# Linear attention on one core: denominators over nine columns, and numerators written into the state's PSUM bank

## The chip, the cores and the metric

The kernel runs on one NeuronCore of a Trainium2 chip. The metric is the time of the device in microseconds (us), the median of several runs. Engines are named as in the profile: PE (TensorE, matmuls), PEld (its weight loads), DVE (VectorE), ACT (ScalarE), POOL (GpSimd), SP (SyncE, which here only starts DMAs). L12 is line 12 of the kernel before. One execution was also recorded by the hardware profiler, and all rows come from it.

## What is computed

An input of 16 x 256 tokens with 128 features goes through a causal linear attention with 16 heads of 8 features, a residual with a layer norm around it, and then a mixture of experts with one expert chosen for each token. The change touches the attention alone. Of the reference:

```
q = elu(x @ Wq + bq) + 1 ;  k = elu(x @ Wk + bk) + 1 ;  v = x @ Wv + bv
def step(carry, qkv):
    s, z = carry
    s = s + einsum('bhd,bhm->bhdm', k_i, v_i)
    z = z + k_i
    qs = einsum('bhd,bhdm->bhm', q_i, s)
    qz = einsum('bhd,bhd->bh', q_i, z)[..., None]
    return (s, z), qs / (qz + 1e-06)
```

So each token has 128 numerators `qs` and 16 denominators `qz + 1e-06`.

## The kernel before, in words

The 4096 tokens are 32 tiles of 128 (token on the partition). A sequence of the batch is two tiles, an even one and an odd one, and the sums over time start anew with each even tile. The attention stage is an unrolled software pipeline over the tiles `t`; each engine runs its own list `step1(t, u)`, `u = t % 4`, in order, and semaphores alone tie the lists together. For tile `t`:

- ACT norms the tile (`xn`), copies the transposed tile out of PSUM (`xnT`), and after the projection makes the parts of elu (`neg`, `rl`, `ex`) and `v`.
- POOL adds them to `qk` (L446) and multiplies every k with every v of its head to `kv`, 128 x 1024 (L452).
- PE sums over the tokens so far with a triangular matrix `upto`: `z` (L1013) into bank 0 or 1, and the state (L1025), four matmul instructions of 512 columns, into a pair of banks, `ps_s[0]` (banks 2 and 3) for even tiles and `ps_s[1]` (banks 4 and 5) for odd ones. It also transposes (L1032, L1034, L1038), projects (L1044), applies the output projection (L1051, L1053), and for an odd tile brings in what the even tile left behind (L1017 makes the sums, L1058 multiplies them by q into `ps_xT`).
- DVE multiplies q and z (`zq`, L721) and masks the carry of an even tile (L726); inverts the last tile's denominators (`rden`, L730); multiplies q and the state out of PSUM (`prod`, 128 x 1024, L735); makes the LAST tile's output `att` = `num` x `rden` (L745); then sums `zq` by heads to `den` (L752) and `prod` to `num` (L757). An even tile ends with `rden` = `den` + 1e-6 (L762), an odd one with `rden` = `den` + 1e-6 + carry (L766) and `num` += carry (L771).

DVE's steps are counted by `s_chain`, six for each tile (`CH = 6`), and its `att` by `s_att`. Each tile's order on PE, in the code's words: z (L1013), carry sums for an even tile (L1017), state (L1025), transposes, projection of tile t + 2 (L1044), output projection of tile t - 2, the carried product for an odd tile (L1058). Before the state of tile t PE waits for DVE to have read the bank pair, that is for the `prod` of tile t - 2:

```
pe.wait_ge(s_kv, t + 1)
at_least(pe, s_chain, CH * (t - 2) + S_READ[odd])
```

In the last tiles (28 and 30) DVE's list is interleaved with steps of the next stage (`prepare_steps`, three between any two of its own; their small operations are the lines from L93 to L124, on `scratch`). Then come the shared network with the routing and, from about 240 us, the experts; neither is touched. POOL starts with writing indices and zeros, in part before a DMA that SP issues.

Of the kernel before, what the change touches and what calls it, by code (L numbers as in the profile page):

```python
# [137 lines left out]
def build(nc, x, w_att, b_qkv, bo, w_ffn, gate_up, down, out):  # L138
    B, S, D = out.shape
    NH = 16  # L140
    HD = D // NH
# [4 lines left out]
    NT = NTOK // P  # L146
# [6 lines left out]
    KVW = NH * HD * HD  # L153
    CW = D + NH
# [13 lines left out]
    with ExitStack() as ctx:  # L168
        def sb(name, shape, dt=F32):
            return ctx.enter_context(nc.sbuf_tensor(name, shape, dt))  # L170

        def sem(name):
            return ctx.enter_context(nc.semaphore(name))
# [46 lines left out]
        qk = sb("qk", [P, 4, 2 * D])  # L220
# [1 line left out]
        qT = sb("qT", [P, D])  # L222
        carry = sb("carry", [P, CW])
        kv = sb("kv", [P, 4, KVW])
        zq = sb("zq", [P, D])
        den = sb("den", [P, NH])
        rden = sb("rden", [P, NH])
        prod = sb("prod", [P, KVW])
        num = sb("num", [P, D])
        att = sb("att", [P, 2, D])  # L230
        attT = sb("attT", [P, D])
# [70 lines left out]
        s_bias_left = sem("bias_left_made")  # L302
        s_mask_series = sem("mask_steps")
        s_bias_rows = sem("bias_rows_written")
        s_norm1 = sem("norm1_ready")
        s_xn = sem("xn_ready")
        s_xn_t = sem("xn_transposed")
# [63 lines left out]
        s_fin_last = sem("last_outputs_ready")  # L371
        s_out = sem("output_stored")

        CH = 6

        Z_READ, S_READ = [2, 1], [3, 2]
        SN = RSTD_STEPS + 1
# [50 lines left out]
        def _(pool):  # L428
# [5 lines left out]
            nc.gpsimd.iota(head_start[:, D:CW], [[HD, NH]], 0, 0, **whole).then_inc(s_iota, 1)  # L434
            nc.gpsimd.iota(row_start[:], [[0, 1]], 0, P, **whole).then_inc(s_iota, 1)
            nc.gpsimd.memset(bias_rows[:], 0.0).then_inc(s_bias_clear, 1)
            nc.gpsimd.memset(rows[:, NT:ST, :], 0.0).then_inc(s_zero, 1)
            nc.gpsimd.iota(rows[:, 0:NT, TOKEN], [[-P, NT]], NTOK, -1, **whole)
            nc.gpsimd.memset(rows[:, 0:NT, TOKEN + 1], 0.0)
# [208 lines left out]
        def _(dve):  # L648
# [63 lines left out]
            def step1(t, u, others=iter(()), between=3):  # L712
                def other(count=between):

                    for _ in range(count):
                        next(others, None)
                multiplied = S_READ[u % 2]
                if live(t, NT):

                    dve.wait_ge(s_z, t + 1)  # L720
                    nc.vector.tensor_tensor(zq[:], ps_qkv[u % 2][:, 3 * D:4 * D], qk[:, u, 0:D],  # L721
                                            ALU.mult).then_inc(s_chain, 1)
                    other()
                if u % 2 == 0 and live(t, NT):

                    nc.vector.tensor_tensor(carry[:], ps_qkv[0][:, 0:CW], head_mask[:], ALU.mult).then_inc(s_chain, 1)  # L726
                    other()
                if live(t - 1, NT):
                    dve.wait_ge(s_chain, CH * (t - 1) + S_READ[1 - u % 2] + 3)
                    nc.vector.reciprocal(rden[:], rden[:]).then_inc(s_recip, 1)  # L730
                    other()
                if live(t, NT):

                    dve.wait_ge(s_s, t + 1)
                    nc.vector.tensor_tensor(  # L735
                        prod[:].rearrange("p (h m d) -> p h m d", h=NH, m=HD),
                        ps_s[u % 2][:].rearrange("p (h m d) -> p h m d", h=NH, m=HD),
                        qk[:, u, 0:D].rearrange("p (h o d) -> p h o d", h=NH, o=1).to_broadcast([P, NH, HD, HD]),
                        ALU.mult).then_inc(s_chain, 1)
                    other()  # L740
                if live(t - 1, NT):
                    dve.wait_ge(s_recip, t)
                    dve.wait_ge(s_chain, CH * t)
                    at_least(dve, s_att_t, t - 2)
                    nc.vector.tensor_tensor(att[:, 1 - u % 2, :].rearrange("p (h m) -> p h m", h=NH),  # L745
                                            num[:].rearrange("p (h m) -> p h m", h=NH),
                                            rden[:].rearrange("p (h o) -> p h o", o=1).to_broadcast([P, NH, HD]),
                                            ALU.mult).then_inc(s_att, 1)
                    other()
                if live(t, NT):  # L750
                    dve.wait_ge(s_chain, CH * t + Z_READ[u % 2])
                    nc.vector.tensor_reduce(den[:], zq[:].rearrange("p (h d) -> p h d", h=NH), AX,  # L752
                                            ALU.add).then_inc(s_chain, 1)
                    other()
                    dve.wait_ge(s_chain, CH * t + multiplied)
                    at_least(dve, s_att, t)
                    nc.vector.tensor_reduce(num[:], prod[:].rearrange("p (n d) -> p n d", d=HD), AX,  # L757
                                            ALU.add).then_inc(s_chain, 1)
                    other()
                    dve.wait_ge(s_chain, CH * t + multiplied + 1)  # L760
                    if u % 2 == 0:
                        nc.vector.tensor_scalar(rden[:], den[:], EPS_DEN, None, ALU.add).then_inc(s_chain, 1)  # L762
                        other()
                    else:
                        dve.wait_ge(s_carried, t + 1)
                        nc.vector.scalar_tensor_tensor(out=rden[:], in0=den[:], scalar=EPS_DEN,  # L766
                                                       in1=ps_xT[:, 3 * D:2 * D + CW],
                                                       op0=ALU.add, op1=ALU.add).then_inc(s_chain, 1)
                        other()
                        dve.wait_ge(s_chain, CH * t + multiplied + 2)  # L770
                        nc.vector.tensor_tensor(num[:], num[:], ps_xT[:, 2 * D:3 * D], ALU.add).then_inc(s_chain, 1)  # L771
                        other()
                other(99)

# [228 lines left out]
        def _(pe):  # L1003

            def step1(t, u):
                odd = u % 2
                if live(t, NT):

                    pe.wait_ge(s_qk, t + 1)
                    pe.wait_ge(s_v, t + 1)  # L1010
                    if isinstance(t, int) and t == 0:
                        pe.wait_ge(s_const, 4)
                    ins = nc.tensor.matmul(ps_qkv[u % 2][:, 3 * D:4 * D], upto[:], qk[:, u, D:2 * D],  # L1013
                                           start=True, stop=True)
                    if not odd:

                        ins = nc.tensor.matmul(ps_qkv[0][:, 0:CW], qk[:, u, D:2 * D], vv[:, 0, :],  # L1017
                                               start=True, stop=True)
                    ins.then_inc(s_z, 1)

                    pe.wait_ge(s_kv, t + 1)
                    at_least(pe, s_chain, CH * (t - 2) + S_READ[odd])
                    for half in range(2):
                        cols = slice(half * 512, (half + 1) * 512)
                        ins = nc.tensor.matmul(ps_s[u % 2][:, cols], upto[:], kv[:, u, cols], start=True, stop=True)  # L1025
                    ins.then_inc(s_s, 1)
                if not odd and live(t - 1, NT):
                    pe.wait_ge(s_chain, CH * t)
                if live(t + 3, NT):
                    pe.wait_ge(s_xn, t + 4)  # L1030
                    at_least(pe, s_xnT, t + 3)
# [7 lines left out]
                if live(t + 2, NT):  # L1039
                    pe.wait_ge(s_xnT, t + 3)  # L1040
                    if isinstance(t, int) and t == -2:
                        pe.wait_ge(s_folded, 1)
                    at_least(pe, s_chain, CH * t + Z_READ[odd])
                    nc.tensor.matmul(ps_qkv[u % 2][:, 0:3 * D], xnT[:, u % 2, :], w_qkv,  # L1044
                                     start=True, stop=True).then_inc(s_qkv, 1)
                if live(t - 2, NT):
# [7 lines left out]
                if odd and live(t, NT):  # L1054

                    pe.wait_ge(s_qT, t + 1)
                    pe.wait_ge(s_chain, CH * (t - 1) + Z_READ[0])
# [70 lines left out]
            pe.wait_ge(s_const, 7)  # L1128

            pe.wait_ge(s_xnT, NT)  # L1130
            pe.wait_ge(s_chain, CH * NT)
            step2(-1, 1)
            pe.wait_ge(s_chain, CH * NT)
            pe.wait_ge(s_y_out, NT)
            for g in range(NG):
                step2(g, g % 2)
# [80 lines left out]
```

## Time and profile before

| what | value |
|---|---|
| three runs | 344.0 us median, 342.65 to 344.68 |
| the profiled execution | 344.77 us, its span from the first to the last instruction 342.8 us |
| busy over the span | DVE 286.7 us, PE 269.8 us, POOL 192.5 us, ACT 186.5 us |
| 60 to 80 us, in the attention | PE 19.97, DVE 19.86, POOL 14.86, ACT 12.04 us of 20 |
| attention tiles in steady order | from about 30 to 127 us |

The 1.97 us between the profiled execution's time and its span lie before the first and after the last instruction. A row of the timeline gives start, duration and, in brackets, the idle time before it and what ended it. Durations on DVE include a tail that overlaps the next instruction, so what an instruction costs its queue is the distance to the next one's start. The four matmuls of L1025 stand as one row, whose end is the modelled end of the last of them.

### The profile page before, as it was taken

How to read it: one execution, taken by the hardware profiler on the slowest of the kernel's cores; microseconds unless marked ns; L12 is line 12 of the kernel's file. 1: busy time of each engine (PE TensorE's matmuls, PEld its weight loads, DVE VectorE, ACT ScalarE, POOL GpSimd, SP SyncE). 2: the span in 40 equal slices, each digit the busy share in tenths (PEclk: the TensorE clock that was granted, in tenths of full speed). 3: DMA queues.
4: the chain of work that ended last, by engine and by line, in shares of the span. 5: the costliest groups of instructions: out<-in, count | busy, mean ns of one | idle time of the engine just before them, and what ended most of it. 6: DMA issues, size and time to landing. Idle time of an engine off the chain costs nothing. (4 is left out here: it accounts for less than half of the span.)

```text
span 342.8 us, 6291 instructions
## 1 busy us (share of the span) xinstructions
PE 269.8 (79%) x1481; PEld 186.0 (54%) x1481; DVE 286.7 (84%) x1138; ACT 186.5 (54%) x573; POOL 192.5 (56%) x221
## 2 busy tenths in 40 slices
PE   3439999999998995839888888875999999998000
PEld 1215555555554552524555555543999888988000
DVE  6996999999999999996899988740389999999930
ACT  2524666656564652447666664203899888885000
POOL 5155777786776773300055556760007888888870
PEclk9987999999999999876999999999899999999755
DMA  6999900000000000000011111227940111110000
GB/s 190 376 424 391 409 8 0 2 3 0 2 0 2 2 0 0 0 2 2 0 63 64 63 62 64 95 78 238 354 158 24 31 35 37 40 36 30 26 2 0
DMA packets 13684, 28.39 MB, mean 83 GB/s; under 512 B 1966, under 2 KB 10166, under 8 KB 12626
## 3 DMA queue, kind: packets, MB, share of 16 engines
q1 hardware_dynamic: 10464, 21.57, 17.2%
q0 software_dynamic: 3040, 6.37, 5.5%
q8 instruction: 13, 0.21, 0.3%
q14 instruction: 21, 0.17, 0.2%
q10 hardware_dynamic: 146, 0.07, 0.1%
HBM read 15.38 MB, written 13.60 MB: 85 GB/s over the span
## 5 line engine op out<-in xcount | busy, mean ns | idle before, releaser
L452 POOL TENSOR_TENSOR kv<-qk,vv 128x1024 f32<-128x1024 f32 x32 | 62.4, 1950 | 2.5
L1025 PE MATMUL banks<-kv,upto 128*128 128x512 f32 x128 | 62.6, 612 | 1.3 <-POOL kv L452 1.3
L1164 PE MATMUL banks<-xsT,w_now 128*128 128x128 f32 x376 | 52.6, 284 | 0.3 <-DVE hT_e L964 0.3
L497 POOL DMA_INDIRECT out<-rows,token_i x47 | 46.8, 996 | 9.9 <-issue 8.3
L446 POOL TENSOR_TENSOR qk<-ex,rl 128x256 f32<-128x256 f32 x32 | 23.3, 727 | 47.2 <-ACT ex L553 47.2
L1164 PEld LDWEIGHTS banks<-xsT,w_now 128*128 128x128 f32 x376 | 47.1, 197 | 0.9 <-issue 0.6
L479 POOL DMA_INDIRECT sorted_rows<-rows,slot_i x32 | 31.7, 990 | 25.8 <-DVE slot_i L821 17.7
L735 DVE TENSOR_TENSOR prod<-banks,qk 128x1024 f32<-128x1024 f32 x32 | 38.9, 1216 | 3.5 <-PE banks L1025 2.9
L757 DVE TENSOR_REDUCE num<-prod 128x128 f32<-128x1024 f32 x32 | 38.6, 1207 | 0.3 <-DVE den L752 0.3
L964 DVE TENSOR_TENSOR hT_e<-silu_e,banks 128x256 f32<-128x256 f32 x47 | 19.3, 412 | 18.8 <-ACT silu_e L640 15.3
L1044 PE MATMUL banks<-w_qkvo,xnT 128*128 128x384 f32 x64 | 28.7, 532 | 8.1 <-ACT xnT L535 3.9
L491 POOL TENSOR_TENSOR rows<-rows,yn 128x128 f32<-128x128 f32 x40 | 19.0, 475 | 27.5 <-DVE yn L956 25.8
L1025 PEld LDWEIGHTS banks<-kv,upto 128*128 128x128 f32 x128 | 22.9, 198 | 17.6 <-issue 16.1
L1172 PE MATMUL banks<-w_exp_down,hT_e 128*128 x188 | 29.6, 280 | 1.0 <-DVE rows L981 1.0
L630 ACT ACTIVATE xs<-rows 128x128 f32<-128x128 f32 x47 | 23.2, 494 | 11.5 <-SPq L421 11.5
L644 ACT COPY w_now<-w_exp 128x512 f32 x47 | 28.7, 610 | 0.0
L535 ACT COPY xnT<-banks 128x128 f32<-128x128 f32 x32 | 8.5, 264 | 34.3 <-PE banks L1032 20.0
L1172 PEld LDWEIGHTS banks<-w_exp_down,hT_e 128*128 128x128 f32 x188 | 24.7, 191 | 1.5 <-issue 1.4
L640 ACT ACTIVATE silu_e<-banks 128x256 f32<-128x256 f32 x47 | 18.0, 383 | 11.8 <-PE banks L1164 11.1
L1120 PE MATMUL banks<-w_ffn,hT 128*128 128x128 f32 x128 | 16.4, 281 | 9.5 <-DVE hT L831 9.5
L528 ACT ACTIVATE xn<-rows,nm,rs 128x128 f32<-128x128 f32 x32 | 16.4, 517 | 10.3 <-DVE nm L122 10.3
L1120 PEld LDWEIGHTS banks<-w_ffn,hT 128*128 128x128 f32 x128 | 14.9, 191 | 11.2 <-DVE hT L831 11.2
(161 smaller groups left out, 647.8 us busy)
## 6 DMA issues: line engine op xcount, KB each, us to landing
sorted_rows<-rows SPq DMA_DIRECT2D x3, 1950.0 KB, 13.4
rows<-sorted_rows SPq DMA_DIRECT2D x10, 520.0 KB, 6.3
w_exp<-in_gate_up SPq DMA_DIRECT2D x4, 1024.0 KB, 20.3
w_exp_down<-in_down SPq DMA_DIRECT2D x4, 512.0 KB, 20.4
rows<-in_x SPq DMA_DIRECT2D x1, 1024.0 KB, 11.0
rows<-sorted_rows SPq DMA_DIRECT2D x2, 390.0 KB, 4.7
rows<-in_x SPq DMA_DIRECT2D x1, 768.0 KB, 8.2
out<-rows,token_i POOLq DMA_INDIRECT x47
```

Of the source, the lines that this page charges most:

```text
L446: nc.gpsimd.tensor_tensor(qk[:, u, :], ex[:, u % 2, :], rl[:, u % 2, :], ALU.add).then_inc(s_qk, 1)
L452: nc.gpsimd.tensor_tensor(kv[:, u, :].rearrange("p (h m d) -> p h m d", h=NH, m=HD), k, v, ALU.mult).then_inc(s_kv, 1)
L479: nc.gpsimd.indirect_dma_start(out=sorted_rows, out_offset=bass.IndirectOffsetOnAxis(ap=slot_i[:, t:t + 1], axis=0), in_=rows[:, t, :], in ...
L497: nc.gpsimd.indirect_dma_start(out=out_rows, out_offset=bass.IndirectOffsetOnAxis(ap=token_i[:, j - 1:j], axis=0), in_=rows[:, j - 1, 0:D] ...
L644: nc.scalar.copy(w_now[:, u % 2, :], flat(w_exp[:, bass.ds(e, 1), :])).then_inc(s_wn, 1)
L735: nc.vector.tensor_tensor(prod[:].rearrange("p (h m d) -> p h m d", h=NH, m=HD), ps_s[u % 2][:].rearrange("p (h m d) -> p h m d", h=NH, m=HD),
L757: nc.vector.tensor_reduce(num[:], prod[:].rearrange("p (n d) -> p n d", d=HD), AX, ALU.add).then_inc(s_chain, 1)
L1025: ins = nc.tensor.matmul(ps_s[u % 2][:, cols], upto[:], kv[:, u, cols], start=True, stop=True)
L1044: nc.tensor.matmul(ps_qkv[u % 2][:, 0:3 * D], xnT[:, u % 2, :], w_qkv, start=True, stop=True).then_inc(s_qkv, 1)
L1120: ins = nc.tensor.matmul(into, hT[:, f, k * P:(k + 1) * P], w_d[:, f, :], start=f == 0, stop=f == FC - 1)
L1164: ins = nc.tensor.matmul(ps_gue[u % 2][:, c * P:(c + 1) * P], w_now[:, u % 2, c * P:(c + 1) * P], xsT[:, u % 2, :], start=True, stop=True)
L1172: ins = nc.tensor.matmul(ps_ye[u % 2][:, 0:D], hT_e[:, u % 2, c * P:(c + 1) * P], flat(w_exp_down[:, bass.ds(e, 1), c, :]), start=c == 0, ...
```

## The change

- `zq` becomes 2 x 16 heads x 9 columns, the ninth written once with 1e-6 by POOL at the start; `den` sums nine columns, so 1e-6 is in it. The addition of 1e-6 (L762) is gone, and for even tiles the reciprocal reads `den`. For odd tiles L766 becomes a plain addition of the carry in PSUM.
- The numerators are no longer left in `num` in SBUF: the sum of an even tile is written to the first 128 columns of the tile's own state bank (`summed`), and for an odd tile the sum goes to `num` and the addition of the carry writes to the state bank. `att` reads them from there.
- `prod` and `zq` have two buffers, one for even and one for odd tiles.
- An even tile has five counted steps and an odd tile six, by `steps_before(t)` in place of `CH * t`.
- Since the numerators of tile t - 2 now sit in the bank pair that the state of tile t overwrites, PE waits for the `att` of tile t - 2 instead of its `prod`.

```
+            nc.gpsimd.memset(zq[:, :, :, HD:HD + 1], EPS_DEN).then_inc(s_eps, 1)
             nc.gpsimd.memset(rows[:, NT:ST, :], 0.0).then_inc(s_zero, 1)
...
+        def steps_before(t):
+
+            return 11 * (t // 2) + 5 * (t % 2)
...
+                summed, summed_last = ps_s[u % 2][:, 0:D], ps_s[1 - u % 2][:, 0:D]
...
-                    nc.vector.tensor_tensor(zq[:], ps_qkv[u % 2][:, 3 * D:4 * D], qk[:, u, 0:D],
+                    nc.vector.tensor_tensor(zq[:, u % 2, :, 0:HD],
...
-                    dve.wait_ge(s_chain, CH * (t - 1) + S_READ[1 - u % 2] + 3)
-                    nc.vector.reciprocal(rden[:], rden[:]).then_inc(s_recip, 1)
+                    dve.wait_ge(s_chain, steps_before(t - 1) + (4 if u % 2 else 5))
+                    nc.vector.reciprocal(rden[:], (den if u % 2 else rden)[:]).then_inc(s_recip, 1)
...
-                        prod[:].rearrange("p (h m d) -> p h m d", h=NH, m=HD),
+                        prod[:, u % 2, :].rearrange("p (h m d) -> p h m d", h=NH, m=HD),
...
-                                            num[:].rearrange("p (h m) -> p h m", h=NH),
+                                            summed_last.rearrange("p (h m) -> p h m", h=NH),
...
-                    nc.vector.tensor_reduce(den[:], zq[:].rearrange("p (h d) -> p h d", h=NH), AX,
+                    nc.vector.tensor_reduce(den[:], zq[:, u % 2, :, :], AX,
...
-                    nc.vector.tensor_reduce(num[:], prod[:].rearrange("p (n d) -> p n d", d=HD), AX,
+                    nc.vector.tensor_reduce(num[:] if u % 2 else summed, prod[:, u % 2, :].rearrange("p (n d) -> p n d", d=HD), AX,
...
-                    if u % 2 == 0:
-                        nc.vector.tensor_scalar(rden[:], den[:], EPS_DEN, None, ALU.add).then_inc(s_chain, 1)
...
-                        nc.vector.scalar_tensor_tensor(out=rden[:], in0=den[:], scalar=EPS_DEN,
-                                                       in1=ps_xT[:, 3 * D:2 * D + CW],
-                                                       op0=ALU.add, op1=ALU.add).then_inc(s_chain, 1)
...
-                        nc.vector.tensor_tensor(num[:], num[:], ps_xT[:, 2 * D:3 * D], ALU.add).then_inc(s_chain, 1)
+                        nc.vector.tensor_tensor(rden[:], ps_xT[:, 3 * D:2 * D + CW], den[:], ALU.add).then_inc(s_chain, 1)
...
+                        nc.vector.tensor_tensor(summed, num[:], ps_xT[:, 2 * D:3 * D], ALU.add).then_inc(s_chain, 1)
...
-                    at_least(pe, s_chain, CH * (t - 2) + S_READ[odd])
+                    at_least(pe, s_att, t - 1)
```

## Rows read from the trace of the kernel before

**Rows 1.** The page: busy time by engine.

```profile
PE 269.8 (79%) x1481; PEld 186.0 (54%) x1481; DVE 286.7 (84%) x1138; ACT 186.5 (54%) x573; POOL 192.5 (56%) x221
```

**Rows 2.** Windows: start:end, length, busy of PE, PEld, DVE, ACT, POOL, clock, DMA.

```profile
60.00:80.00 20.00, 19.97 (x89) 11.56 (x89) 19.86 (x48) 12.04 (x47) 14.86 (x13) 1.00 0.01 2
120.00:140.00 20.00, 15.70 (x61) 9.16 (x60) 19.43 (x57) 9.06 (x34) 11.48 (x9) 0.91 0.00 0
```

**Rows 3.** Timeline of tiles 16 (even), 17 (odd) and the start of 18.

```profile
83.45 0.27 PE L1032 MATMUL banks<-ident,xn 128*128 128x128 f32 x1
...
83.66 1.22 DVE L735 TENSOR_TENSOR prod<-banks,qk 128x1024 f32<-128x1024 f32 x1
...
84.80 0.28 DVE L745 TENSOR_TENSOR att<-num,rden 128x128 f32<-128x128 f32 x1
...
84.88 1.88 PE L1025 MATMUL banks<-kv,upto 128*128 128x512 f32 x4
...
86.32 0.16 DVE L762 TENSOR_SCALAR rden<-den 128x16 f32<-128x16 f32 x1
86.36 1.95 POOL L452 TENSOR_TENSOR kv<-qk,vv 128x1024 f32<-128x1024 f32 x1
86.39 0.28 DVE L721 TENSOR_TENSOR zq<-banks,qk 128x128 f32<-128x128 f32 x1
...
86.80 1.23 DVE L735 TENSOR_TENSOR prod<-banks,qk 128x1024 f32<-128x1024 f32 x1
...
87.94 0.53 DVE L745 TENSOR_TENSOR att<-num,rden 128x128 f32<-128x128 f32 x1
...
88.81 1.88 PE L1025 MATMUL banks<-kv,upto 128*128 128x512 f32 x4
...
89.82 0.29 DVE L771 TENSOR_TENSOR num<-num,banks 128x128 f32<-128x128 f32 x1
...
90.73 1.22 DVE L735 TENSOR_TENSOR prod<-banks,qk 128x1024 f32<-128x1024 f32 x1
```

**Rows 4.** Timeline of tiles 22 to 24.

```profile
104.87 1.23 DVE L735 TENSOR_TENSOR prod<-banks,qk 128x1024 f32<-128x1024 f32 x1
...
107.58 1.95 POOL L452 TENSOR_TENSOR kv<-qk,vv 128x1024 f32<-128x1024 f32 x1
...
107.89 1.67 DVE L762 TENSOR_SCALAR rden<-den 128x16 f32<-128x16 f32 x1
...
109.47 0.28 DVE L721 TENSOR_TENSOR zq<-banks,qk 128x128 f32<-128x128 f32 x1
...
109.90 0.88 PE L1044 MATMUL banks<-w_qkvo,xnT 128*128 128x384 f32 x2 [1.59 <-DVE zq L721]
...
113.58 1.23 DVE L735 TENSOR_TENSOR prod<-banks,qk 128x1024 f32<-128x1024 f32 x1 [0.18 <-PE banks L1025]
```

**Rows 5.** Timeline of the last tiles, 28 to 31.

```profile
129.52 1.88 PE L1025 MATMUL banks<-kv,upto 128*128 128x512 f32 x4
...
131.00 1.95 POOL L452 TENSOR_TENSOR kv<-qk,vv 128x1024 f32<-128x1024 f32 x1
131.09 2.02 DVE L745 TENSOR_TENSOR att<-num,rden 128x128 f32<-128x128 f32 x1
...
133.03 0.15 DVE L108 SCALAR_TENSOR_TENSOR scratch<-scratch 128x4 f32<-128x4 f32 x1
...
135.72 1.16 DVE L735 TENSOR_TENSOR prod<-banks,qk 128x1024 f32<-128x1024 f32 x1
```

**Rows 6.** Timeline of the start, 16 to 22 us.

```profile
16.97 1.95 POOL L452 TENSOR_TENSOR kv<-qk,vv 128x1024 f32<-128x1024 f32 x1
...
18.97 1.98 PE L1025 MATMUL banks<-kv,upto 128*128 128x512 f32 x4 [1.29 <-POOL kv L452]
...
19.68 1.95 POOL L452 TENSOR_TENSOR kv<-qk,vv 128x1024 f32<-128x1024 f32 x1
19.70 1.97 DVE L96 SCALAR_TENSOR_TENSOR scratch<-scratch 128x28 f32<-128x28 f32 x1
```

More of the change, by code:

```diff
@@ L224, in build @@
         kv = sb("kv", [P, 4, KVW])
-        zq = sb("zq", [P, D])
+        zq = sb("zq", [P, 2, NH, HD + 1])
         den = sb("den", [P, NH])
         rden = sb("rden", [P, NH])
-        prod = sb("prod", [P, KVW])
+        prod = sb("prod", [P, 2, KVW])
         num = sb("num", [P, D])
@@ L304, in build @@
         s_bias_rows = sem("bias_rows_written")
+        s_eps = sem("denominator_eps_written")
         s_norm1 = sem("norm1_ready")
@@ L372, in build @@
         s_out = sem("output_stored")
-        CH = 6
+        def steps_before(t):
+            return 11 * (t // 2) + 5 * (t % 2)
         Z_READ, S_READ = [2, 1], [3, 2]
@@ L717, in step1 @@
                 multiplied = S_READ[u % 2]
+                summed, summed_last = ps_s[u % 2][:, 0:D], ps_s[1 - u % 2][:, 0:D]
                 if live(t, NT):
                     dve.wait_ge(s_z, t + 1)
-                    nc.vector.tensor_tensor(zq[:], ps_qkv[u % 2][:, 3 * D:4 * D], qk[:, u, 0:D],
+                    nc.vector.tensor_tensor(zq[:, u % 2, :, 0:HD],
+                                            ps_qkv[u % 2][:, 3 * D:4 * D].rearrange("p (h d) -> p h d", h=NH),
+                                            qk[:, u, 0:D].rearrange("p (h d) -> p h d", h=NH),
                                             ALU.mult).then_inc(s_chain, 1)
@@ L742, in step1 @@
                     dve.wait_ge(s_recip, t)
-                    dve.wait_ge(s_chain, CH * t)
+                    dve.wait_ge(s_chain, steps_before(t))
                     at_least(dve, s_att_t, t - 2)
                     nc.vector.tensor_tensor(att[:, 1 - u % 2, :].rearrange("p (h m) -> p h m", h=NH),
-                                            num[:].rearrange("p (h m) -> p h m", h=NH),
+                                            summed_last.rearrange("p (h m) -> p h m", h=NH),
                                             rden[:].rearrange("p (h o) -> p h o", o=1).to_broadcast([P, NH, HD]),
@@ L750, in step1 @@
                 if live(t, NT):
-                    dve.wait_ge(s_chain, CH * t + Z_READ[u % 2])
-                    nc.vector.tensor_reduce(den[:], zq[:].rearrange("p (h d) -> p h d", h=NH), AX,
+                    dve.wait_ge(s_chain, steps_before(t) + Z_READ[u % 2])
+                    if t == 0:
+                        dve.wait_ge(s_eps, 1)
+                    nc.vector.tensor_reduce(den[:], zq[:, u % 2, :, :], AX,
                                             ALU.add).then_inc(s_chain, 1)
@@ L754, in step1 @@
                     other()
-                    dve.wait_ge(s_chain, CH * t + multiplied)
+                    dve.wait_ge(s_chain, steps_before(t) + multiplied)
                     at_least(dve, s_att, t)
-                    nc.vector.tensor_reduce(num[:], prod[:].rearrange("p (n d) -> p n d", d=HD), AX,
+                    nc.vector.tensor_reduce(num[:] if u % 2 else summed, prod[:, u % 2, :].rearrange("p (n d) -> p n d", d=HD), AX,
                                             ALU.add).then_inc(s_chain, 1)
@@ L759, in step1 @@
                     other()
-                    dve.wait_ge(s_chain, CH * t + multiplied + 1)
-                    if u % 2 == 0:
-                        nc.vector.tensor_scalar(rden[:], den[:], EPS_DEN, None, ALU.add).then_inc(s_chain, 1)
+                    if u % 2:
+                        dve.wait_ge(s_chain, steps_before(t) + multiplied + 1)
+                        dve.wait_ge(s_carried, t + 1)
+                        nc.vector.tensor_tensor(rden[:], ps_xT[:, 3 * D:2 * D + CW], den[:], ALU.add).then_inc(s_chain, 1)
@@ L763, in step1 @@
                         other()
-                    else:
-                        dve.wait_ge(s_carried, t + 1)
-                        nc.vector.scalar_tensor_tensor(out=rden[:], in0=den[:], scalar=EPS_DEN,
-                                                       in1=ps_xT[:, 3 * D:2 * D + CW],
-                                                       op0=ALU.add, op1=ALU.add).then_inc(s_chain, 1)
-                        other()
-                        dve.wait_ge(s_chain, CH * t + multiplied + 2)
-                        nc.vector.tensor_tensor(num[:], num[:], ps_xT[:, 2 * D:3 * D], ALU.add).then_inc(s_chain, 1)
+                        dve.wait_ge(s_chain, steps_before(t) + multiplied + 2)
@@ L1027, in step1 @@
                 if not odd and live(t - 1, NT):
-                    pe.wait_ge(s_chain, CH * t)
+                    pe.wait_ge(s_chain, steps_before(t))
                 if live(t + 3, NT):
@@ L1042, in step1 @@
                         pe.wait_ge(s_folded, 1)
-                    at_least(pe, s_chain, CH * t + Z_READ[odd])
+                    at_least(pe, s_chain, steps_before(t) + Z_READ[odd])
                     nc.tensor.matmul(ps_qkv[u % 2][:, 0:3 * D], xnT[:, u % 2, :], w_qkv,
@@ L1056, in step1 @@
                     pe.wait_ge(s_qT, t + 1)
-                    pe.wait_ge(s_chain, CH * (t - 1) + Z_READ[0])
+                    pe.wait_ge(s_chain, steps_before(t - 1) + Z_READ[0])
                     nc.tensor.matmul(ps_xT[:, 2 * D:2 * D + CW], qT[:], carry[:], start=True, stop=True
@@ L1130, in _ @@
             pe.wait_ge(s_xnT, NT)
-            pe.wait_ge(s_chain, CH * NT)
+            pe.wait_ge(s_chain, steps_before(NT))
             step2(-1, 1)
-            pe.wait_ge(s_chain, CH * NT)
+            pe.wait_ge(s_chain, steps_before(NT))
             pe.wait_ge(s_y_out, NT)
```

## The prediction, made before the changed kernel was built or run

> **What bounds the kernel now.** I read the page first: DVE is the busiest engine with 286.7 us, PE has 269.8 [rows 1]. That invites the reading "DVE bounds, so less work on DVE is time saved". The windows by stage spoil it: from 60 to 80 us PE is busy for 19.97 of 20 us and DVE for 19.86 [rows 2], so in the attention the totals cannot tell which of the two sets the pace. The timeline of one pair of tiles can [rows 3]. The state of tile 17 runs on PE from 84.88 to 86.76, and DVE's prod of tile 17 starts at 86.80. The state of tile 18 ends at 88.81 + 1.88 = 90.69 and its prod starts at 90.73. Both times DVE's longest product starts 0.04 us after the end of the state: PE releases it. No idle time is shown on DVE because the tail of its earlier instruction covers the wait. A pair takes 90.73 - 83.66 = 7.07 us, 3.14 us from the even prod to the odd one and 3.93 us from there to the next even one.
>
> The third view is a slip. At 107.89 DVE's addition of epsilon takes 1.67 us, PE then sits idle for 1.59 us before L1044, and the way from even prod to even prod is 113.58 - 104.87 = 8.71 us in place of 7.07 [rows 4]. So 1.59 us of idle PE lengthened the pair by 1.64 us: an idle PE is passed on whole. This is what I price the change with. From tile 28 on it is otherwise: DVE has steps of the next stage between its own, PE is busy for 15.70 of 20 us only [rows 2], and DVE sets the pace.
>
> **The change part by part.**
>
> Epsilon in a ninth column. It takes L762 from DVE's queue, 86.39 - 86.32 = 0.07 us in an undisturbed even tile [rows 3], and adds 16 elements of 144 to the sum of zq; by the 1.22 us of prod for 1024 elements [rows 3] that is about 0.02. In the steady tiles DVE has to wait for PE anyway, so I cost both at nothing; the cover is the wait for the state, and without it the gain would be 0.05 x 13 = 0.7 us. The write of the column is one small instruction of POOL at the start, ahead of zeros that let SP's clearing DMA begin. No row shows one like it; it lies between 0 and 0.28 us, what DVE's rows of 128 elements take [rows 3]. POOL's first product starts only at 16.97 [rows 6], and the DMA behind it fills a buffer that the experts use after 160 us. I take 0. Writing zq with a gap after each 8 elements is not in the trace either: between 0 and, if it halved the rate, about 0.14 us for 128 elements on DVE, behind the same cover. I take 0. DVE's wait for the column at tile 0 is for something written some 15 us before, and the second buffers of zq and prod move no instruction: 0 as well.
>
> Numerators read from PSUM by att. In tile 17's step att starts at 87.94 and takes 0.53 us, against 0.28 at 84.80; POOL's kv runs until 86.36 + 1.95 = 88.31 in the first case [rows 3]. The slip is the same thing: POOL's kv runs until 109.53, and L762, begun 0.31 us after it, ends at 109.56 [rows 4]. At 131.09 att begins 0.09 us after a kv and takes 2.02 us [rows 5]. These DVE instructions have all their operands in SBUF; prod, whose state operand is in PSUM, starts at 86.80 in the middle of the same kv and takes its usual 1.23 us [rows 3]. So the new att should take 0.28 us always. What it gives: 0.53 - 0.28 = 0.25 us in each odd step, under the cover of PE's pace up to tile 27, in the open for the last one, which leads into DVE's own stage.
>
> The Trainium skill says the same of the mechanism ("SBUF — State Buffer", Who interferes with whom): a DVE instruction with two SBUF inputs and a GpSimd instruction that reads SBUF exclude one another, one with at most one SBUF input does not contend. The trace agrees, and L96 shows it for a fused operation too, 1.97 us beside the kv that began at 19.68 [rows 6]. Another rule of it speaks against the change ("VectorE: DVE Perf Modes", The TRN2 errata): a PSUM source has 62 cycles more of fixed cost than an SBUF source, about 0.065 us at 0.96 GHz. Here L771, with an operand in PSUM, takes 0.29 us against att's 0.28 [rows 3], so I add 0.01 at most; by the page's figure 13 x 0.065 = 0.8 us would come on top of the sum below.
>
> The slip goes. L762, which fell behind kv at 107.89, is gone. Whatever made L762 fall behind kv there and not at 86.32 may come again, but then meets slack on DVE. I take -1.64 us, with 0 as the other bound, since not every run need have had it.
>
> The new wait. The state of tile 17 now needs att of tile 15, which is DVE's instruction right after the prod of tile 16. That prod starts 0.04 us after the state of tile 16 ended, and att at 84.80 ends at 85.08 [rows 3]. PE is ready at 84.88, when it starts this matmul today. What lies between the end of a releaser and the state's start: at 18.97 the state began 0.05 us after kv's end at 18.92 and took 1.98 in place of 1.88, together 0.15 [rows 6]. The slowest that I find is L1044, which starts at 109.90, 0.15 us after the end of zq at 109.47 + 0.28 = 109.75 [rows 4]; with the same lengthening of 0.10 that is 0.25. I take 0.15: 85.08 + 0.15 - 84.88 = 0.35 us. The bounds are 0.25 (0.05 for the release) and 0.45 (0.25 for it). Nothing makes it up: PE's work is in order, behind the waiting state stand the transposes, L1044 and all that ACT and POOL make of it, and DVE's next prod waits for just this state. The loop is closed, state, prod, att, state, so a faster DVE elsewhere doesn't bring it back. DVE will then idle before the odd prod, which moves from 3.14 to 3.49 us after the even one.
>
> For an even tile the wait is covered. Att of tile 16 starts at 87.94, ends at 88.22 without POOL's hindrance, plus 0.15 is 88.37, while PE gets to the state of tile 18 at 88.81 [rows 3]: 0.44 us to spare.
>
> It counts for the odd tiles 3, 5, ... 27, whose predecessors' prod PE releases: 13 x 0.35 = +4.6 us. Tile 1 has nothing to wait for. Tile 29's state, at 129.52 now, moves behind att of 27 (131.09 + 0.28 + 0.15 = 131.52) and ends at 133.40, before its prod at 135.72 [rows 5]: covered by 2.3 us of DVE's steps; tile 31's likewise.
>
> The last tiles, where DVE sets the pace. Saved: 0.25 of the last hindered att of the steady part; L762 twice, 0.07 each; and of the 2.02 us at 131.09 little, because the next steps (L108 at 133.03) have their operands in SBUF too and would run into the same kv until 132.95: L108 would end soon after 132.95 where it now ends at 133.18, about 0.20 earlier. Together 0.25 + 0.14 + 0.20 = -0.6 us. Bounds 0 and -2.1 (if all of 2.02 - 0.28 = 1.74 came free, with the rest). The sums and additions that now write PSUM stand in the open here; no row writes PSUM from DVE, and I take no difference; the bounds are 0.07 either way for each of the few that lie in the open, the difference between the two durations of prod, 1.16 and 1.23 [rows 3, 5].
>
> The sum: +4.6 - 1.6 - 0.6 = +2.4 us. On the profiled execution of 344.77 us (span 342.8, 1.97 around it, unchanged) that is 347.2; it stood 0.8 above the median of the runs shown, so on 344.0 it is **346.4 us**.
>
> **The rivals.**
>
> A, the other side: the new wait is free. The place is the state of odd tiles; it would need att's release 0.35 us earlier, or PE to have 0.35 us of idle time ahead of its state that I took for work. Below a stall of 2.2 / 13 = 0.17 us the gains decide. Then 344.0 - 1.6 - 0.6 = 341.8 us. Against it: the two releases at 0.04 us and the slip that was passed on whole. For it: DVE's row shows hardly any idle time, so DVE and PE may share the pace. Chance 0.13.
>
> B: the wait costs more. The place is the same; the release is as slow as L1044's (0.25) and att slower from PSUM by the 0.07 of the two kinds of prod, and the slip is not in the usual run: 13 x (0.45 + 0.07) = 6.8, less 0.6: 350.2 us. Chance 0.12. It would also hold if PE's extra idle time lowered its clock, which is granted in full (1.00) at 60 to 80 us and is 0.91 where PE idles at 120 to 140 [rows 2]; 0.35 us in 7.4 is far less idle time than there.
>
> C, my forecast, a stall of 0.25 to 0.45 us that outweighs the gains: 344.0 + 3.3 - 2.2 = 345.1 at its low end, 344.0 + 5.9 - 0.6 = 349.3 without the slip's gain. Chance 0.75.
>
> **How the numbers follow.** A measurement tells about 0.5% (1.7 us) from no change. Slower by more than that means above 345.7: of C's 0.75 about 0.56, and all of B, 0.68. Faster means below 342.3: nearly all of A and a trace of C, 0.12. Within: 0.20. The range is 343.8 to 349.2: C whole, with what the tail may give beyond 0.6 down to 345.1 - 1.3; A and most of B are left out, with about 0.2.
>
> **What would show it.** Odd states released by att instead of running on from z, and idle PE of 0.3 to 0.4 us before them; 7.4 us from even prod to even prod; att at 0.28 to 0.30 us in all tiles; idle time on DVE before prod; no DVE instruction of the attention above 1.3 us in the steady part; DVE's first step of tile 28 with its lead won. The forecast is wrong if pairs still take 7.07 us, or if even states wait too.

## The result, and the profile of the changed kernel

The changed kernel takes 350.12 us in the median (348.07 to 350.95, four runs), the kernel before 344.05 in the same comparison: a ratio of 1.0173 with a 95% interval of 1.0116 to 1.0230. In a second comparison it took 350.57 us against 343.73, ratio 1.0187 (1.0127 to 1.0247). So it is slower by 6 to 7 us: the direction that was forecast, but more than twice the size (+2.4 us), and outside the range that ended at 349.2.

The page's first line of the changed kernel, and two stretches of its windows in the order of [rows 2]:

```profile
PE 276.6 (80%) x1481; PEld 187.8 (54%) x1481; DVE 282.9 (81%) x1122; ACT 186.1 (54%) x573; POOL 192.7 (55%) x222
```

```profile
60.00:80.00 20.00, 19.40 (x87) 11.09 (x85) 18.28 (x43) 12.00 (x48) 13.96 (x11) 1.00 0.01 2
120.00:140.00 20.00, 16.03 (x61) 8.61 (x60) 17.71 (x48) 7.71 (x31) 11.23 (x9) 0.87 0.00 1
```

DVE has 3.8 us less to do than in [rows 1], and yet the kernel is slower. In the steady tiles both engines that were full in [rows 2] now have gaps. The timeline of tiles 16 to 18, which answers to [rows 3] (L1029 is the state, L1025 before; L742 prod, L752 att):

```profile
85.90 1.23 DVE L742 TENSOR_TENSOR prod<-banks,qk 128x1024 f32<-128x1024 f32 x1 [0.28 <-PE banks L1029]
...
86.90 0.39 PE L1017 MATMUL banks<-qk,upto 128*128 128x128 f32 x2
87.04 0.28 DVE L752 TENSOR_TENSOR att<-banks,rden 128x128 f32<-128x128 f32 x1
...
87.44 0.30 PEld L1029 LDWEIGHTS banks<-kv,upto 128*128 128x128 f32 x2 [0.34 <-issue]
...
87.47 1.96 PE L1029 MATMUL banks<-kv,upto 128*128 128x512 f32 x4 [0.18 <-DVE att L752]
...
89.46 1.22 DVE L742 TENSOR_TENSOR prod<-banks,qk 128x1024 f32<-128x1024 f32 x1 [0.45 <-PE banks L1029]
...
90.61 0.28 DVE L752 TENSOR_TENSOR att<-banks,rden 128x128 f32<-128x128 f32 x1
...
91.47 1.88 PE L1029 MATMUL banks<-kv,upto 128*128 128x512 f32 x4
...
93.39 1.22 DVE L742 TENSOR_TENSOR prod<-banks,qk 128x1024 f32<-128x1024 f32 x1 [0.28 <-PE banks L1029]
```

The odd state at 87.47 is released by att, the even one at 91.47 runs on. (The idle time of 0.18 us in the brackets is less than the delay, since the row of the matmul before it overlaps. The state starts 0.57 us after the start of L1017 at 86.90, where in the kernel before it was 0.23, and its row is 0.08 us longer: 0.42 us together.) From the even prod to the odd one it is 89.46 - 85.90 = 3.56 us in place of 3.14, from there to the next even one 3.93 as before; a pair takes 7.49 us. All pairs from tile 4 to tile 26 take 7.49 or 7.50, and no slip is among them. The waits from 45 to 120 us say it from both sides (us in all, times, longest):

```profile
DVE prod L742 <- PE banks L1029: 7.7, 21, 0.4
...
PE banks L1029 <- DVE att L752: 1.8, 10, 0.2
```

The last tiles answer to [rows 5]:

```profile
132.16 1.22 DVE L742 TENSOR_TENSOR prod<-banks,qk 128x1024 f32<-128x1024 f32 x1
...
133.90 1.96 POOL L456 TENSOR_TENSOR kv<-qk,vv 128x1024 f32<-128x1024 f32 x1
134.07 1.80 DVE L106 TENSOR_TENSOR scratch<-scratch 128x4 f32<-128x4 f32 x1
135.80 0.28 DVE L752 TENSOR_TENSOR att<-banks,rden 128x128 f32<-128x128 f32 x1
...
136.22 3.75 PE L1029 MATMUL banks<-kv,upto 128*128 128x512 f32 x4 [3.65 <-DVE att L752]
...
140.01 1.23 DVE L742 TENSOR_TENSOR prod<-banks,qk 128x1024 f32<-128x1024 f32 x1 [1.30 <-PE banks L1029]
```

Att itself is no longer held by POOL, but L106, a step of the next stage that stands ahead of it and has its operands in SBUF, is, for 1.80 us. PE waits 3.65 us for att, and then the four matmuls of the state take 3.75 us where they took 1.88: twice as long. The window over the time of these four matmuls shows a granted clock of 0.50, the lower of its two levels:

```profile
136.22:139.97 3.75, 3.75 (x5) 1.58 (x6) 2.38 (x9) 0.00 (x0) 0.00 (x0) 0.50 0.00 0
```

DVE's prod waits another 1.30 us for them. From the prod of tile 28 to that of tile 29 it is 7.85 us in place of 6.68.

With the starts of prod in tiles 2 and 28 and of the first `hT` of the next stage as marks, the two profiled executions differ thus:

| stretch | before, us | changed, us | difference |
|---|---|---|---|
| to prod of tile 2 | 34.09 | 33.47 | -0.6 |
| prod of tile 2 to 28 | 94.95 | 98.69 | +3.7 |
| prod of 28 to first hT | 31.98 | 34.19 | +2.2 |
| from there to the end of the span | 181.8 | 181.3 | -0.5 |

The first and the last line are no effect of the change: over the 14 traces of this study prod of tile 2 starts between 32.6 and 34.7 us, and the end takes 180.8 to 183.9 us, whatever the edit. The second line is 13 x 0.42 = 5.5 for the wait, less 1.64 for the slip. The third line is not all at tile 29. Of its 2.2 us, 1.17 lie before prod of tile 29, 0.45 between that and prod of tile 30, 0.05 before prod of tile 31 and 0.54 behind it; in the second traces of both kernels (experiments eleven and twelve) it is 0.78, -0.13, 0.42 and 0.88. Behind prod of tile 31 the delay is seen on ACT: its copies for tile 31 wait for transposes that stand behind the late state, and its next long step (`ya`) starts 1.35 us after that prod, where it was 0.25 us ahead of it in the kernel before and is 0.14 us behind it in experiment six. The two lines together leave 5.9 us for the attention, close to the 6.1 us of the medians.

### The profile page after: what moved, and what is told of

Read it like the earlier page. It is cut to its first block and busy times, and to the rows that moved or that the text cites. A ratio compares the mean times of both kernels' runs of the same rounds, so it can differ in the third digit from the quotient of the medians.

```text
span 347.6 us, 6277 instructions
## 1 busy us (share of the span) xinstructions
PE 276.6 (80%) x1481; PEld 187.8 (54%) x1481; DVE 282.9 (81%) x1122; ACT 186.1 (54%) x573; POOL 192.7 (55%) x222
## 5 line engine op out<-in xcount | busy, mean ns | idle before, releaser
L1029 PE MATMUL banks<-kv,upto 128*128 128x512 f32 x128 | 67.3, 652 | 9.9 <-DVE att L752 9.1
L742 DVE TENSOR_TENSOR prod<-banks,qk 128x1024 f32<-128x1024 f32 x32 | 39.1, 1223 | 12.3 <-PE banks L1029 12.3
L1029 PEld LDWEIGHTS banks<-kv,upto 128*128 128x128 f32 x128 | 23.8, 206 | 30.1 <-issue 25.2
L766 DVE TENSOR_REDUCE banks<-prod 128x128 f32<-128x1024 f32 x16 | 19.5, 1218 | 0.0
```

Source lines behind the costliest of these rows:

```text
L742: nc.vector.tensor_tensor(prod[:, u % 2, :].rearrange("p (h m d) -> p h m d", h=NH, m=HD), ps_s[u % 2][:].rearrange("p (h m d) -> p h m d" ...
```

## The experiments

All were timed beside the kernel before. "Tail" below is the stretch from prod of tile 28 to the first hT, in the one profiled execution of each kernel; such an execution can lie anywhere among the runs of its kernel, so traces say where time goes and the medians how much.

**One: nine columns and two buffers alone.**

```
-                summed, summed_last = ps_s[u % 2][:, 0:D], ps_s[1 - u % 2][:, 0:D]
+                summed, summed_last = num[:], num[:]
...
-                    at_least(pe, s_att, t - 1)
+                    at_least(pe, s_chain, steps_before(t - 2) + S_READ[odd])
```

> The changed kernel with its numerators left in num in SBUF and PE's old wait (for the prod of tile t - 2); the ninth column, the two buffers and the new counting stay. If the new wait of the state is what costs: pairs of tiles at 7.07 us again, the odd state running on from z, 3.14 us from even prod to odd prod, the slip of tiles 22 to 24 gone, about 342.5 us. If the cost lies in DVE's new forms (the gaps in zq, the nine columns, the first write by POOL): pairs stay near 7.49 us and the time near 350.

Measured: 343.65 us against 344.1, ratio 0.9992 (0.9965 to 1.0019). Even to odd 3.16 us, pairs of 7.09, no slip, tail 31.94. This half of the change is free: the gaps in zq and the nine columns cost 0.02 us a pair. Its profiled execution has the slip's gain in it (93.56 us from tile 2 to 28 in place of 94.95), but the medians differ by 0.45 us only, and the interval reaches from 1.2 us faster to 0.7 slower.

**Two: the wait alone.**

```
-                    at_least(pe, s_chain, CH * (t - 2) + S_READ[odd])
+                    at_least(pe, s_att, t - 1)
```

> The kernel before with one line changed: PE waits for the att of tile t - 2 instead of its prod, everything else as before. If the wait is the whole cost: odd states released by att, 3.56 us from even prod to odd prod, pairs of 7.49 us, 13 x 0.42 = 5.5 us in the steady tiles and 1 to 2 us in the last ones, since att of tile 27 comes after a kv of POOL: 350 to 352 us. If numerators in PSUM cost by themselves: clearly less than 349.

Measured: 349.42 us, ratio 1.0161 (1.0126 to 1.0195). Pairs of 7.49 us, tail 34.28. This one line, with nothing in PSUM that needs it, gives 5.3 of the 6.1 us. That is less than the 350 to 352 that I expected, and less than its trace gives (99.93 us from tile 2 to 28 and 34.28 of tail, 7.3 us more than before); the profiled execution was the slowest of the four, and the 2 us between the two readings stay open. Its last tiles read like those of the changed kernel:

```profile
136.17 1.80 DVE L106 TENSOR_TENSOR scratch<-scratch 128x4 f32<-128x4 f32 x1
137.89 0.28 DVE L745 TENSOR_TENSOR att<-num,rden 128x128 f32<-128x128 f32 x1
...
138.31 3.75 PE L1025 MATMUL banks<-kv,upto 128*128 128x512 f32 x4 [3.64 <-DVE att L745]
```

**Three: the upper half of the state first.** The numerators lie in the lower bank of the pair; only that one needs att.

```
-                    at_least(pe, s_att, t - 1)
-                    for half in range(2):
+                    at_least(pe, s_chain, steps_before(t - 2) + S_READ[odd])
+                    for half in (1, 0):
+                        if half == 0:
+                            at_least(pe, s_att, t - 1)
```

> The changed kernel, but PE computes the state's upper 512 columns first, behind the old wait, and waits for att only before the lower 512 columns, whose bank holds the numerators. By the wait's theory the upper half (0.86 us) covers the 0.42 us: pairs of 7.07 us, no idle time of PE before the state, 342 to 343 us if the last tiles follow. If PE were held by something else of the change (PSUM traffic of DVE, the order of releases), pairs stay at 7.49 us.

Measured: 342.9 us, ratio 0.9974 (0.9939 to 1.0008), 7 us below the changed kernel. The odd state starts at once and all four matmuls run on, although att is at work until 84.35:

```profile
83.92 0.39 PE L1017 MATMUL banks<-qk,upto 128*128 128x128 f32 x2
84.07 0.28 DVE L752 TENSOR_TENSOR att<-banks,rden 128x128 f32<-128x128 f32 x1
84.14 1.88 PE L1031 MATMUL banks<-kv,upto 128*128 128x512 f32 x4
```

Pairs of 7.07 us, tail 32.39. All else of the change is in here, PSUM writes and reads of DVE too; the loss is gone with the wait. In the last tiles att is as late as before, and PE still idles for 2.70 us, but only half of the state is left to do, and PE does it at full clock (1.00). The lower clock comes later, at the projection behind the next wait, which takes 1.62 us in place of 0.81 at a granted clock of 0.50:

```profile
128.58 1.80 DVE L106 TENSOR_TENSOR scratch<-scratch 128x4 f32<-128x4 f32 x1
...
130.30 0.28 DVE L752 TENSOR_TENSOR att<-banks,rden 128x128 f32<-128x128 f32 x1
...
130.63 1.12 PE L1031 MATMUL banks<-kv,upto 128*128 128x512 f32 x2 [2.70 <-DVE att L752]
...
133.20 1.62 PE L1050 MATMUL banks<-w_qkvo,xnT 128*128 128x384 f32 x2 [1.22 <-DVE zq L726]
```

**Four: att ahead of prod.** The block of DVE's list that makes `att` of tile t - 1 is moved in front of the one that makes `prod` of tile t.

```
+                if live(t - 1, NT):
+                    dve.wait_ge(s_recip, t)
...
+                                            ALU.mult).then_inc(s_att, 1)
                 if live(t, NT):
 
                     dve.wait_ge(s_s, t + 1)
```

> The changed kernel with DVE's att of the last tile placed before the prod of the current one. By the wait's theory att is then done before the even state ends, the odd state doesn't wait, DVE has 6.5 us of work in a pair of 7.07: 342 to 343 us. The tile-29 state is then released before DVE's interleaved steps too. If DVE sets the pace after all, the att ahead of prod delays each prod by 0.2 to 0.3 us and pairs become 7.3 us or longer: 345 us or more.

Measured: 342.82 us, ratio 0.9975 (0.9946 to 1.0004). Pairs of 7.07 us with 3.16 from even to odd, no slip, tail 31.4. The wait is in the text of the program and costs nothing, since what it waits for comes before the prod that PE's last state releases. The tail isn't quite comparable here: prod of tile 28 itself comes 9.10 us after that of tile 26, where it is 8.40 in experiment three.

**Five: no steps between prod and att in the last tiles.**

```
                         ALU.mult).then_inc(s_chain, 1)
-                    other()
+                    other(0 if t in (28, 30) else between)
```

> The changed kernel; in tiles 28 and 30 DVE takes none of the next stage's steps between prod and att (they come later). Theory: in the last tiles the wait costs about 1.8 us because the interleaved steps let att of tiles 27 and 29 come late, one of them held by POOL's kv. Then att comes 1.14 us after prod, tile 29's state starts about 1.6 us after prod of 28 instead of 4.1, its end is covered again, prod 28 to prod 29 falls from 7.85 to about 6.5 us and the time by 1.3 to 1.8 us to about 348.4. Pairs of the steady tiles stay at 7.49. Rival, that the last tiles lose by DVE's writes to PSUM: no change, 350.

Measured: 349.01 us, ratio 1.0133 (1.0083 to 1.0183). The steady pairs stay at 7.49 us; prod 28 to prod 29 takes 6.26 us, and the tail 31.59 in place of 34.19. The medians give only 1.1 us of these 2.6, and the intervals of the two ratios overlap, so that this mend works is read from the trace. L106 is still held for 1.80 us, now behind att:

```profile
134.51 0.28 DVE L752 TENSOR_TENSOR att<-banks,rden 128x128 f32<-128x128 f32 x1
...
134.94 1.95 PE L1029 MATMUL banks<-kv,upto 128*128 128x512 f32 x4 [1.15 <-DVE att L752]
...
135.29 1.80 DVE L106 TENSOR_TENSOR scratch<-scratch 128x4 f32<-128x4 f32 x1
```

**Six: the late att, with PE kept busy.**

```
+                    if t in (29, 31):
+                        at_least(pe, s_chain, steps_before(t - 2) + S_READ[odd])
+                        for _ in range(4):
+                            nc.tensor.matmul(ps_s[1][:, 512:1024], upto[:], kv[:, u, 512:1024], start=True, stop=True)
                     at_least(pe, s_att, t - 1)
```

> The changed kernel; while PE waits for att before the states of tiles 29 and 31 it does the upper half of the state four times over (its result is overwritten by the same values), 3.4 us of matmuls for nothing. Att comes as late as before. If the half clock after PE's idle time is what uncovers the wait, the state of tile 29 takes 1.88 us instead of 3.75, DVE's wait of 1.30 us before its prod disappears, and the time falls by 1.3 us to about 348.8. If lateness alone does it, the prod of tile 29 stays 7.85 us behind that of 28 and the time at 350.

Measured: 346.39 us, ratio 1.0071 (1.0039 to 1.0104). Att ends 3.91 us after the start of prod of tile 28, as in the changed kernel (3.92), but the state takes 1.98 us, at a granted clock of 1.00 (last line):

```profile
132.20 1.22 DVE L742 TENSOR_TENSOR prod<-banks,qk 128x1024 f32<-128x1024 f32 x1
132.45 3.60 PE L1029 MATMUL banks<-kv,upto 128*128 128x512 f32 x8
...
135.83 0.28 DVE L752 TENSOR_TENSOR att<-banks,rden 128x128 f32<-128x128 f32 x1
...
136.17 1.98 PE L1033 MATMUL banks<-kv,upto 128*128 128x512 f32 x4
...
138.66 1.16 DVE L742 TENSOR_TENSOR prod<-banks,qk 128x1024 f32<-128x1024 f32 x1
```

```profile
136.17:138.15 1.98, 1.98 (x6) 0.95 (x6) 1.84 (x8) 0.00 (x0) 0.00 (x0) 1.00 0.00 0
```

The rival that lateness alone does it is out: with the clock kept, prod of tile 29 doesn't wait (6.46 us after that of 28) and the tail is 31.67. Experiment five shows the other half: an att that isn't late mends it as well. To uncover the wait it takes both, lateness and the lower clock. The gain of 3.7 us on the changed kernel is larger than the 2.1 to 2.5 us that the traces give; the rest I can't place.

**Seven: prod to num in one piece in the last tiles**, on top of three: `other(0 if t in (28, 30) else between)` also behind att and den.

> The version with the upper half first, and in tiles 28 and 30 none of the next stage's steps between prod, att, den and num, which POOL's kv cannot hold up; they come after num. The 1.80 us for which kv holds the step L106 should shrink to about 1.0 us, since 2.7 us of it are filled with work that kv does not hinder: from prod 28 to the first hT 31.4 to 31.9 us instead of 32.4, total 342.2 against 342.9. Rival: the norm's steps come later, ACT gets its scales later, and the time stays or rises by 0.5 us.

Measured: 341.57 us, ratio 0.9938 (0.9909 to 0.9967). The tail is 31.81 us in place of 32.39, and the longest hold by POOL 1.03 us (at L101) in place of 1.80 (at L106). The interval of the ratio overlaps that of experiment three, so the gain is shown by the trace only.

**Eight: attT before qT**, on top of three: in ACT's list the block that copies `attT` moves in front of the one that copies `qT`.

> The version with the upper half first, and ACT copies attT before qT in odd steps. If PE sets the pace of the steady tiles, then the only idle time left on it, about 0.17 us in each odd step before L1055 where it waits for attT, goes: pairs of 6.9 us instead of 7.07, 14 x 0.17 = 2.3 us, about 340.6 us, faster than both kernels. If DVE sets the pace (it was at 19.86 of 20 us before), pairs stay at 7.07 and the time at 342.9.

Measured: 339.54 us, ratio 0.9857 (0.9819 to 0.9895), also clearly below that of experiment three. Pairs of 6.90 us. L1057 is the first matmul behind the wait for `attT`; in the odd step it starts 0.65 us after the start of the projection (L1050, at 85.96) where it was 0.83 in experiment three:

```profile
82.69 1.23 DVE L742 TENSOR_TENSOR prod<-banks,qk 128x1024 f32<-128x1024 f32 x1
...
86.61 0.23 PE L1057 MATMUL banks<-bias_rows,ones_bf 128*128 128x128 bf16 x1
...
89.59 1.23 DVE L742 TENSOR_TENSOR prod<-banks,qk 128x1024 f32<-128x1024 f32 x1
```

**Nine: seven and eight together.**

> The version with the upper half first, attT before qT, and the last tiles' prod to num in one piece. The three lie in different places, so they should add: pairs of 6.90 us and 31.8 us from prod 28 to the first hT, 342.9 - 3.4 - 1.3 = 338.2 us. If the last tiles' mend only moves a wait, it stays at 339.5.

Measured: 338.8 us, ratio 0.9864 (0.9816 to 0.9912), pairs of 6.90 us, tail 31.13. The effects add in the trace; against eight alone the runs don't tell them apart.

**Ten: attT before qT in the kernel before.**

> The kernel before with attT copied before qT, nothing else. If PE sets the pace and DVE was just behind it (6.88 us of its queue in a pair of 7.07), pairs fall to between 6.90 and 6.95 us and the time to about 341.5: then the change's savings on DVE were worth nothing and are worth at most 0.05 us a pair even with the faster PE. If DVE set the pace, pairs stay at 7.07 and the time at 344.

Measured: 343.26 us, ratio 0.9997 (0.9963 to 1.0031). No gain, the second of the two outcomes, and an instructive one: the pairs stay at 7.07 us (3.27 and 3.80). PE now waits in the even step, ahead of a matmul where it didn't before:

```profile
81.60 0.30 DVE L726 TENSOR_TENSOR carry<-banks,head_mask 128x144 f32<-128x144 f32 x1
...
82.04 0.88 PE L1044 MATMUL banks<-w_qkvo,xnT 128*128 128x384 f32 x2
...
83.32 1.88 PE L1025 MATMUL banks<-kv,upto 128*128 128x512 f32 x4
```

L1044 overwrites the bank that carry reads, so it starts 0.14 us after carry's end at 81.90, with a row of 0.88 us like the late one of [rows 4]. Before the edit the same two stand 0.22 us apart. There is a second loop of the same length as PE's: prod of an odd tile, the held att of 0.53 us, den, num, the carry, L1044, state, prod of the next odd tile. By the rows it is 3.43 us from prod to carry, 0.30 for carry, 0.14 to L1044 and 3.20 from there to the next odd prod, 7.07 in all. L762 isn't in it; the held att is, and costs 0.25 us more of it than one that isn't held. That this is what makes the difference to experiment eight is worked out from the rows; no edit tried it alone.

**Eleven and twelve: the two kernels once more.**

> The changed kernel once more, beside the others. 350 us; pairs 7.49 us, and if the last tiles' loss is the late att and the half clock and not chance, again a prod of tile 29 about 7.8 us after that of 28 and a state of tile 29 at half clock.

> The kernel before once more. If the slip of tiles 22 to 24 belongs to the program and not to the one execution, it stands in this trace at the same tile: one addition of epsilon of about 1.7 us and a pair of 8.7 us.

The changed kernel repeats itself: 350.57 us, pairs of 7.49, prod 28 to prod 29 in 7.46 us, tail 33.73, the state of tile 29 in 3.38 us. The kernel before took 344.44 us in a single run, again with one addition of epsilon of 1.67 us, at 107.67, and a pair of 8.71 us in the same place. The slip stood there in all four traces of kernels that have L762 (before, two, ten, twelve), each time at tile 22 with num late by 0.33 to 0.34 us just before it (0.26 of it shown as idle time of DVE), and in none of the ten without it. What delays num there wasn't tried. That the slip is in every trace and its 1.64 us hardly in the medians of experiment one stays open.

## Why the prediction was wrong

**Right.** PE releases prod, an idle PE is passed on, the odd states wait and the even ones don't, 13 of them; att takes 0.28 us from PSUM at all times; the slip goes; prod gets idle time in front of it. Experiments two to four show that the loss is the wait: alone it makes it, and without it, with all else kept, it is gone. Rival A falls by them. Rival B, "350.2 us", named the measured time by luck. Its release of 0.25 us was near the measured 0.23, but its att slowed by PSUM isn't so (0.28 us), the slip that it leaves in is gone from the traces (though the medians of experiment one hardly show the gain), and it knew nothing of the last tiles.

**A term too small: the release.** "I take 0.15" should have been 0.23: att ends at 87.32, the state starts at 87.47 and its row is 0.08 longer. The row that I took it from was a release by POOL; that by DVE in [rows 4], my upper bound, was the nearer one. The stall is 0.42 us in place of 0.35, and 13 x 0.07 = 0.9 us more.

**The step that failed: tile 29.** "Tile 29's state ... moves behind att of 27 (131.09 + 0.28 + 0.15 = 131.52) and ends at 133.40, before its prod at 135.72: covered by 2.3 us of DVE's steps". The prod was to start 6.68 us after that of tile 28, the state to end 4.36 us after it. In the changed kernel the state starts 4.06 us after that prod and ends at 7.81. Two things were wrong in it. I let kv hold only what stands behind att, when a small shift of the queues (kv starts 1.74 us after prod of tile 28, it was 1.96) put L106 into its way ahead of att, so att ended 3.92 us after the start of prod of tile 28, where I had 2.33 (131.37 against 129.04), 1.6 us later. And I priced the state at 1.88 us behind an idle time of PE that I had myself just made long; it ran at the lower clock. I had looked at the clock for the steady tiles only, where the gaps are short and it indeed stays at 1.00. The kernel before had a warning in this very place, 1.11 us for a projection that takes 0.81 in the steady tiles, at a granted clock of 0.74:

```profile
135.78 1.11 PE L1044 MATMUL banks<-w_qkvo,xnT 128*128 128x384 f32 x2 [2.29 <-DVE zq L721]
```

Experiments five and six each take away one of the two, and each brings the tail back, from 34.19 to 31.6 us. They do so at tile 31 as well, whose "likewise" failed with tile 29: its state starts after 3.21 us of idle time, runs at a granted clock of 0.57, and ends just before its prod begins (in the second trace that prod waits 0.31 us).

**The gain of the last tiles.** "-0.6 us" counted L762 twice and what att no longer spends. Without the exposed wait the tail is 32.39 us in experiment three against 31.98 before: +0.4, not the -0.34 that I had in this stretch. The hold by POOL is handed to another instruction, 1.80 us long in place of att's 2.02. Prod of tile 29 does come 0.23 us sooner (6.45 in place of 6.68); what is lost lies behind it, 6.83 us to prod of tile 30 in place of 6.31, where PE has a granted clock of 0.59 in place of 0.73 and DVE waits for it twice, 0.23 and 0.46 us (once, 0.25 us, in the kernel before). Whether the clock is the whole of it wasn't tried apart; with the clock at 1.00, in experiment six, the same stretch takes 6.09. Nor did the 0.25 us ahead of tile 28 appear: from prod 26 to prod 28 it is 8.40 us in experiment three and 8.39 in the kernel before; there L93, the first of the next stage's steps with operands in SBUF, is now held, 0.48 us long where it took 0.26.

**The sum again.** +5.5 - 1.6 + 2.2 = +6.1 us by the traces' terms, where I had +4.6 - 1.6 - 0.6 = +2.4. Here 5.5 and 1.6 are the steady tiles and 2.2 is the tail. That the sum meets the medians is in part luck: the slip's 1.6 is hardly seen in the medians of experiment one, and those of experiment two show 2 us less than its trace.

**Two small ones, without effect.** The ninth column is written at 1.84 us and first summed at 26.21, some 24 us later and not 15; and the upper end of C is 349.3, where the range stops at 349.2.

**A premise that held only half.** "In the steady tiles DVE has to wait for PE anyway", with 0.7 us as the worth without that cover. Experiment ten says that DVE's loop through the carry was as long as PE's. The change's work on DVE was worth nothing in the kernel before, because PE was in the way, and what mends PE was worth nothing, because DVE's held att was. With both, pairs go from 7.07 to 6.90 us, 13 x 0.17 = 2.2 us, and with the slip gone eight is 3.7 us below ten in the medians (3.6 from tile 2 to 28 in the traces). The change wasn't worthless: it freed DVE and put the wait in PE's way.

## What to carry to other kernels

When a buffer gets a second tenant, price the release of the buffer, not the instruction saved: find which loop (here state, prod, att, state) the new wait closes, and try whether the part of the buffer that isn't shared can go first. Where two engines are both full, a saving on one shows nothing by itself; look for the loop through each before calling it hidden. A cover computed in one stretch has to be checked there, with the operations as they will fall and at the clock that PE will have after its idle time.

## What was not expected of the hardware

- After 3.65 us of idle time PE ran the state at half its rate throughout (3.75 us in place of 1.88, granted clock 0.50; 3.38 us and 0.57 in the second trace of the same kernel). After 2.70 us in experiment three the two matmuls took 1.12 us at a clock of 1.00, but the projection behind another 1.22 us of idle time took 1.62 at 0.50: the last gap alone doesn't tell the clock. With matmuls in the gap whose result is overwritten, the state took 1.98 us at 1.00.
- A DVE instruction with all operands in SBUF that stands 0.17 us behind the start of a kv of POOL costs 1.80 us, and moving one such instruction to PSUM hands the hold to the next (L106, or L101 in experiment seven). The Trainium skill ("SBUF — State Buffer", Who interferes with whom) calls the port pair that the two share an exclusive lock. The traces agree for a kv that came first: L106 ends at 135.87, kv at 135.86. No run here shows the other order. The same section of the Trainium skill excepts modes in which DVE uses both ports when it says that an instruction with one SBUF input doesn't contend; the prediction left the exception out, and L762, with one such input, was held for 1.67 us [rows 4].
- DVE's sums and additions written to PSUM cost hardly more than those to SBUF: L766 has 1.218 us on average into PSUM and 1.209 into SBUF, between 45 and 120 us:

```profile
L766 DVE TENSOR_REDUCE banks<-prod 128x128 f32<-128x1024 f32 x10 | 12.2, 1218 | 0.0
L766 DVE TENSOR_REDUCE num<-prod 128x128 f32<-128x1024 f32 x10 | 12.1, 1209 | 0.0
```
